# Order of small copies on ScalarE and VectorE in the group loop of a fused attention and feed-forward kernel

## What is computed

```
xn  = layernorm(x) * g_norm
q   = l2norm(xn @ Wq) per head (16 heads of 64) * q_scale
k,v = xn @ Wkv (one head of 64 each), a null key and value in front
k   = l2norm(k) * k_scale
sim = 8 * q @ k^T + bias(i - j), causal, masked     # bias from a small MLP
out = softmax(sim) @ v
y   = layernorm(out @ Wout) * g_out
x   = x + FFN(y)     # int8 fake-quantised gate, up and down products, SiLU
```

## Time and profile before

| | us |
|---|---|
| median of 3 runs | 286.36 (286.25 to 287.96) |
| the profiled execution, its own time | 287.82 |
| its span | 285.9 |
| mean granted clock of TensorE, share of full speed | 0.975 |
| TensorE, VectorE, ScalarE, GpSimd busy in the span | 260.6, 234.4, 223.5, 201.3 |

### The profile page before, as it was taken

The page is one execution under the profiler, slowest core; times in us unless marked ns, Lnnn a source line. Parts: engine busy times, 40 slices in busy tenths (PEclk is TensorE's granted clock), DMA queues, the critical chain, the costliest instruction groups (busy, mean ns, idle before and its releaser), DMA issues.

```text
span 285.9 us, 7418 instructions
## 1 busy us (share of the span) xinstructions
PE 260.6 (91%) x2209; PEld 209.4 (73%) x2210; DVE 234.4 (82%) x973; ACT 223.5 (78%) x778; POOL 201.3 (70%) x395
## 2 busy tenths in 40 slices
PE   6889989999999999999999999999999999978261
PEld 5467768888788888888888888888888877752060
DVE  6699887998789888988898889787977787879893
ACT  3577878988898889888988898889888898358380
POOL 6485887887788778878887888778877785013310
PEclk9999999999999999999999999999999999999757
DMA  4746000000000000000000000000000200000004
GB/s 127 187 140 162 1 2 1 2 3 0 3 0 5 0 3 0 2 1 3 0 2 3 2 0 2 1 3 0 2 1 3 62 17 3 0 3 2 1 23 128
DMA packets 12109, 6.48 MB, mean 23 GB/s; under 512 B 1614, under 2 KB 11939, under 8 KB 12068
## 3 DMA queue, kind: packets, MB, share of 16 engines
q1 hardware_dynamic: 11642, 5.78, 7.8%
q10 hardware_dynamic: 426, 0.20, 0.2%
HBM read 4.88 MB, written 1.07 MB: 21 GB/s over the span
## 4 chain that ended last, share of the span: by engine, by line
PE 50%; DVE 17%; ACT 15%; POOL 8%; issue 7%; DMA 1%; DVEq 0%; POOLq 0%; ACTq 0%
PE bank L979 11%; ACT prob L633 8%; PE bank L930 7%; POOL rq L450 6%; PE back L1022 4%; PE front L956 4%; PE front L1022 4%; PE bank L793 4%; DVE score L1379 3%; PE back L956 3%; DVE qn L1243 3%; PE bank L811 3%; DVE qn L1237 2%; ACT sq L580 2%; DVE oT L1369 2%
## 5 line engine op out<-in xcount | busy, mean ns | idle before, releaser
L633 ACT ACTIVATE prob<-score,negmax 128x258 f32<-128x258 f32 (+1 forms) x256 | 113.9, 453 | 27.0 <-DVE negmax L1379 26.9
L491 POOL TENSOR_SCALAR prob<-prob,rrow 128x258 f32<-128x258 f32 x254 | 105.7, 436 | 22.2 <-DVE rrow L1387 19.2
L450 POOL TENSOR_TENSOR rq<-qn,neghalf 128x8 f32<-128x8 f32 x32 | 53.9, 1684 | 2.7
L979 PE MATMUL bank<-pT,val 128*64 128x256 f32 x496 | 49.9, 336 | 0.2
L633 ACT ACTIVATION_READ_ACCUMULATOR prob<-score,negmax 128x1 f32 x256 | 49.7, 194 | 0.0
L979 PEld LDWEIGHTS bank<-pT,val 128*64 128x64 f32 x496 | 30.2, 136 | 17.6 <-issue 4.9
L1379 DVE CUSTOM_DVE_ANT_0 score<-front,bias 128x258 f32<-128x258 f32 (+1 forms) x128 | 38.0, 353 | 2.0 <-PE front L956 1.8
L1243 DVE TENSOR_TENSOR qn<-bank,rq 128x512 f32<-128x512 f32 x31 | 21.3, 688 | 22.2 <-POOL rq L450 22.1
L930 PE MATMUL bank<-wout,oT 128*128 128x128 f32 x256 | 36.8, 287 | 2.1 <-DVE oT L1369 1.7
L1379 DVE CUSTOM_DVE_ANT_0 score<-back,bias 128x258 f32<-128x258 f32 (+1 forms) x128 | 37.3, 348 | 0.0
L930 PEld LDWEIGHTS bank<-wout,oT 128*128 128x128 f32 x256 | 30.9, 191 | 7.1 <-DVE oT L1369 5.2
(11 more groups left out here) (228 smaller groups left out, 469.1 us busy)
## 6 DMA issues: line engine op xcount, KB each, us to landing
bias<-relative_table SPq DMA_DIRECT2D x8, 256.0 KB, 4.8
X<-in_x_dram SPq DMA_DIRECT2D x1, 896.0 KB, 5.7
out_dram<-prob SPq DMA_DIRECT2D x3, 256.0 KB, 2.6
prob<-in_L_cond_Wq_dram SPq DMA_DIRECT2D x1, 512.0 KB, 3.7
wout<-in_L_cond_Wout_dram SPq DMA_DIRECT2D x1, 512.0 KB, 5.6
prob<-in_L_ffn_w_down_dram SPq DMA_DIRECT2D x1, 176.0 KB, 4.0
X<-in_x_dram SPq DMA_DIRECT2D x1, 128.0 KB, 2.1
prob<-in_L_ffn_w_gate_dram SPq DMA_DIRECT2D x1, 128.0 KB, 2.1
```

Source lines behind the costliest of these rows:

```text
L450: pool.tensor_tensor(dst, src, neghalf[:, 0:width], ALU.pow).then_inc(done, 1)
L491: pool.tensor_scalar(prob[:, par, h, cols], prob[:, par, h, cols], rrow[:, par, h, t:t + 1], 1.0, ALU.mult, ALU.mult).then_inc(normed, 1)
L633: act.activation(prob[:, par, h, cols], score[:, h % 4, cols], ACT.Exp, scale=-1.0, bias=negmax[:, par, h, t:t + 1], accum_out=rowsum[:, p ...
L979: last = pe.matmul(ps[a * D:a * D + D, pair * N + i0:pair * N + N], val[m % 2][:, blk, :], turned[:, 2 * pair + a, c0:c1], start=blk == 1, ...
```

## The change

Two orders change, and nothing else: no instruction is added, dropped or altered.

- ScalarE, `group`: all four copies of the turned probabilities stand ahead of the small piece (kv, kT, xT or yT); before, copies 2 and 3 stood behind it.
- VectorE, `group`: `oT_copy` stands ahead of `q_normalise` in every group. Before, that was so in group 2 of each batch but the first.

```
--- before.py
+++ after.py
@@ -665,8 +665,8 @@
                 if s.made is not None:
                     q_square(s.made, q_ps)
                 if s.turned is not None:
-                    pT_evac(s.turned, 0)
-                    pT_evac(s.turned, 1)
+                    for i in range(GH):
+                        pT_evac(s.turned, i)
                 if s.kv is not None:
                     kv_evac(s.kv, front_tails)
                 if s.kT is not None:
@@ -675,9 +675,6 @@
                     xT_evac(s.xT, front_tails)
                 if s.yT is not None:
                     yT_evac(s.yT)
-                if s.turned is not None:
-                    pT_evac(s.turned, 2)
-                    pT_evac(s.turned, 3)
                 if s.null is not None:
                     null_evac(s.null)
                 if s.first and s.g == 1:
@@ -1426,11 +1423,10 @@
             def group(s):
                 if s.g == 2 and s.prev is not None:
                     y_normalise(s.prev)
+                if s.summed is not None:
                     oT_copy(s.summed)
                 if s.quarter >= 4:
                     q_normalise(s.quarter, s.quarter % 4, q_ps)
-                if s.summed is not None and not (s.g == 2 and s.prev is not None):
-                    oT_copy(s.summed)
                 if s.at == 1:
                     xT_split_low(1, 1)
                 if s.first:
```

## The result

The changed kernel took 284.13 us (median of 6 runs, 282.75 to 284.63) against 286.35 before (6 runs). The ratio of the runs is 0.9879, 95% interval 0.9844 to 0.9913: 1.2% faster. The forecast was 282.7 with a range of 281.0 to 285.8. The profiled execution took 284.12; 284.2 was forecast for it.

The account below looks back on a forecast made before the run. TensorE was taken to bound the loop, busy 28.21 of 28.28 us a batch. Terms -3.0 + 0.8 - 0.9 - 0.25 - 0.3 = -3.65 took the profiled 287.82 to 284.2; 1.46 lower for the median gave 282.7, range 281.0 to 285.8.

Parts of the forecast that it names:

- (1): Rival that everything goes as forecast: 282.7 us, own range 281.4 to 284.0; chance 0.60.
- Term A: Copies of turned probabilities before the small piece: TensorE's 12 waits before the values' sums close, -3.0 us, bounds 0 and -3.0.
- the chain through rq: Ring rq, q's scaling, oT, scores, exponents, squares, norms: 6.95 us falls to about 6.35, no longer bounding beside TensorE's 7.07.
- Term B: Late kv delays VectorE's k squares and group 1's scores by 0.26, half let through in six batches: +0.8 us, bounds 0 and +1.6.
- C: oT ahead of q's scaling saves TensorE 0.15 before group 3's output products, scores 0.2 earlier: -0.9 us, bounds 0 and -1.2.
- D: First batch: group 3's 0.82 wait for oT goes, group 2's later q scaling costs 0.57: -0.25 us, bounds -0.8 and +0.6.
- E: Last group of the loop: the output products' 0.25 wait goes, with earlier scores behind it: -0.3 us, bounds 0 and -0.8.
- (2): Rival: last copy still ends over 0.73 after the sums' start, so TensorE's wait stays: -0.65, 285.7 us; chance 0.12.
- (3): Rival: TensorE reaches turns 2 and 3 earlier and waits for GpSimd's normalised probabilities: -2.45, 283.9 us; chance 0.12.
- (4): Rival: VectorE's xn blocks GpSimd's short k operations through the shared port, 0.30 in six batches: 284.5 us; chance 0.05.
- (5): Rival, slower: VectorE's late kv wait before k's squares in group 0 passes whole to TensorE: +4.1, 290.5 us; chance 0.05.
- (6): Rival: the order was not what held TensorE, and the same gaps return under another name: 286.3 us; chance 0.06.

## Why the prediction was right or wrong

**The forecast held, and its main mechanism:** TensorE's two gaps in the loop closed but for the 0.04, a batch takes 27.78 (27.7 to 27.9 was forecast), the ending comes earlier, and up to the last sums it is 3.87 us, against 3.65. The profiled execution came within 0.1 of its forecast. The median, 284.13, lies in the range but 1.4 above the 282.7, just above the 281.4 to 284.0 of (1) and above the 283.5 under which the prediction put a chance of 0.60: it took off 1.46 for the step from the profiled execution to the median, a step between the two levels of the last section, and four of the changed kernel's six runs stayed on the level of the profiled one.

**Term A (-3.0) was mis-sized and wrongly set down as the copies' own.** Alone they give 0.15 us from group 2 on. Behind oT's new place they give 211.04 - 208.94 = 2.1. Two causes. In a steady batch the copies give 28.04 - 27.78 = 0.26 behind oT's new place, where 0.24 + 0.21 + 0.04 was counted: with oT first alone the sums take 1.66 in group 2 and 1.59 in group 0, with both changes 1.49, so 0.04 stays lost in each and the 0.04 of group 3 isn't won either. And as long as oT stands behind q's scaling, the chain through rq holds the products back by about as much as the sums end earlier (0.08 + 0.14 + 0.07 for 0.18 + 0.14 in a batch). The prediction saw that chain ("stops being a second bound") but priced it in neither term.

**Term B (+0.8) was 0 in the steady batches**, in its bounds: the late kv's wait of 0.86 is there, the scores of group 1 come 0.17 late instead of 0.26, and GpSimd's normalising still ends 0.1 before TensorE asks. The place was right, as 0.37 us more there show. But kv's copy of the first batch, which no term had, costs 0.30 at TensorE's scores.

**Terms C, D, E (-0.9, -0.25, -0.3)** were too small together: oT's place alone gives 2.06 where 1.45 was counted. In a steady batch it is 28.28 - 28.04 = 0.24 and not 0.15, since group 0 gains too (7.29 to 7.18 with oT first only), which the prediction left in its bounds; and the first of the five gains 0.5 (28.54 to 28.04), which no term had: there one power of q's norms on GpSimd took 1.93 instead of 1.67 (it is as long in every kernel here), and with oT behind q's scaling that went through to TensorE, as the 28.55 of the copies alone in the same batch shows. In D the loss by oT's new place came out as counted, 0.57. For E, the stretch from group 25 to the end falls from 50.17 to 49.25 for all causes.

**That the sum came out is luck:** A's excess of 0.9 and the missing 0.3 of the first batch were made good by B's caution of 0.8 and by the 0.6 that C to E fell short. The single terms should not be quoted.

**The rivals.** (2) is half true: the copies in groups 2, 3 and 0 are 0.04 too late, not 0.2. (3) is one step away, as the later kv shows, but didn't happen. (4) happened in kind, 0.13 us in three batches, and cost nothing. (5) and (6) didn't happen. What no run tried is whether the remaining 0.04 in three groups of four can be had.

## What to carry to other kernels

When the bound engine has two small gaps a period, ask for each whether the path behind the other is as long: closing one alone may give nothing (the copies alone lost 0.16 us here), and both together more than the sum of each alone (3.87 against 1.90). An instruction that only needs the bound engine's last product should not stand behind one that needs a long round trip through three other engines. An order that is right in the steady loop can be wrong in its first round, where rq is ready before the sums are and little covers a late piece: keeping the two old orders there gave another 0.87 us.

## What the runs showed of the hardware

The time of one kernel has two levels some 1.5 to 2 us apart, and they go, not without exceptions, with TensorE's granted clock. Of the changed kernel's runs those at a mean clock of 0.987 took 282.38 and 282.75, and most at 0.975 to 0.977 took 284.1 to 284.9 (one at 0.976 took 282.78; what made it an exception is open). In the last session of the kernel before, four runs at 0.987 took 286.25 to 286.43, and most near 0.975 took 288.0 to 288.6 (two at 0.976 took 286.7 and 286.9). By the means of that session and the changed kernel beside it, the change is worth 3.95 us at 0.987 (one run after) and 3.8 near 0.975. The loop has no part in the levels. The windows view of the changed kernel's end in two executions, first a profile that took 282.38, then the one of 284.12; the first column after POOL's is the granted clock:

```profile
262.00:272.00 10.00, 2.65 (x21) 2.03 (x21) 9.03 (x23) 5.46 (x11) 2.32 (x2) 0.72 0.00 1
272.00:280.60 8.60, 2.90 (x40) 2.46 (x37) 4.77 (x12) 1.84 (x4) 1.27 (x1) 0.90 0.44 126
```

```profile
262.00:272.00 10.00, 2.65 (x21) 2.00 (x21) 8.93 (x23) 5.36 (x11) 2.30 (x2) 0.65 0.00 1
272.00:282.30 10.30, 3.88 (x40) 3.44 (x38) 4.87 (x13) 1.92 (x4) 1.27 (x1) 0.67 0.37 105
```

In both the clock has fallen between 262 and 272 (1.00 is the level of 2.4 GHz, 0.5 would be all at 1.2 GHz), while TensorE is busy 2.65 us of 10; before 262 it is 1.00. In the first execution it is back for most of the last stretch (0.90), in the second not (0.67), and TensorE's work there takes 3.88 us instead of 2.90 while the stretch is 1.7 us longer. The loop itself is at 1.00 throughout in every profile, and its distances agree within 0.12 us between two profiles of one kernel (208.94 and 208.98, 208.37 and 208.48). So small changes of this kernel are read from distances in the trace rather than from medians of a few runs.
